# Weighted sums of both query halves in one bank, copied and turned once per unit; at most one operand load behind a store of maxima

## The reference

```python
scores = jnp.einsum('bhqd,bhkd->bhqk', q, k)          # / sqrt(8), masked
attn = jax.nn.softmax(scores, axis=-1)
out = jnp.einsum('bhqk,bhkd->bhqd', attn, v)
```

## Time and profile before

| what | value |
|---|---|
| median of three runs | 1235.33 us |
| profiled execution | 1236.83 us, its span 1234.9 us |
| TensorE busy | 1122.0 us, 91% |
| VectorE / ScalarE / GpSimd busy | 935.3 / 735.9 / 447.5 us |
| first attention, 188.7 to 687 us | TensorE busy 489.0 of 498.3 us |
| second attention, 776 to 1000 us | TensorE busy 210.5 of 224.0 us |
| granted clock, mean | 0.955 |

### The profile page before, as it was taken

The page is one execution under the profiler, slowest core; times in us unless marked ns, Lnnn a source line. Parts: engine busy times, 40 slices in busy tenths (PEclk is TensorE's granted clock), DMA queues, the critical chain, the costliest instruction groups (busy, mean ns, idle before and its releaser), DMA issues. The chain is left out here.

```text
span 1234.9 us, 22211 instructions
## 1 busy us (share of the span) xinstructions
PE 1122.0 (91%) x7511; PEld 614.9 (50%) x7518; DVE 935.3 (76%) x2098; ACT 735.9 (60%) x1148; POOL 447.5 (36%) x714
## 2 busy tenths in 40 slices
PE   4668879999999999999998697799999989999997
PEld 2345663344444444343443374444444448888874
DVE  7979988688888888888884372877787636777776
ACT  3557640666666666666666453356666667787762
POOL 6002220142323332332222120387776622566630
PEclk9989996899999999999999897799999989999999
DMA  4322790003302130212000013222222253687542
GB/s 137 96 84 64 113 125 2 19 27 108 101 13 93 41 116 23 82 55 85 28 2 2 1 54 86 67 64 61 64 65 61 58 169 127 188 258 245 163 122 83
DMA packets 94975, 103.52 MB, mean 84 GB/s; under 512 B 17217, under 2 KB 72838, under 8 KB 94864
## 3 DMA queue, kind: packets, MB, share of 16 engines
q1 hardware_dynamic: 88928, 93.09, 28.0%
q0 software_dynamic: 4992, 8.48, 2.0%
q10 hardware_dynamic: 944, 0.54, 0.2%
HBM read 64.67 MB, written 38.43 MB: 83 GB/s over the span
## 5 line engine op out<-in xcount | busy, mean ns | idle before, releaser
L1136 ACT ACTIVATE a_probs<-a_pst 128x1024 f32<-128x1024 f32 (+4 forms) x544 | 413.9, 813 | 274.9 <-PE a_pst L1084 274.3
L1160 DVE TENSOR_REDUCE a_tops<-a_ps 128x1 f32<-128x512 f32 (+9 forms) x624 | 340.9, 589 | 84.4 <-PE a_ps L1054 76.6
L992 POOL TENSOR_SCALAR_AFFINE_SELECT a_probs<-a_probs 128x256 f32<-128x256 f32 (+3 forms) x384 | 180.6, 481 | 366.8 <-ACT a_probs L1136 361.4
L1054 PE MATMUL a_ps<-kp,qp 96*128 96x512 bf16 (+9 forms) x1280 | 293.5, 307 | 0.0
L1084 PE MATMUL a_pst<-qp,kp 99*128 99x512 bf16 (+4 forms) x1088 | 259.1, 330 | 15.2 <-DMA qp<-a_top_rows 11.5
L1103 PE MATMUL a_po<-a_probs,vh 128*32 128x512 f32 (+4 forms) x2176 | 232.0, 499 | 2.6 <-POOL a_probs L992 2.5
L1160 DVE TENSOR_REDUCE a_tops_lead<-a_ps 128x1 f32<-128x512 f32 x256 | 161.6, 681 | 5.9 <-PE a_ps L1054 5.6
L1054 PEld LDWEIGHTS a_ps<-kp,qp 96*128 96x128 bf16 x1280 | 111.4, 100 | 79.1 <-DVE a_tops_lead L1160 15.5
L1051 PE MATMUL a_ps<-mask_s,identb 128*128 128x128 bf16 (+8 forms) x624 | 144.1, 234 | 6.8 <-PEq L1254 4.4
L1084 PEld LDWEIGHTS a_pst<-qp,kp 99*128 99x128 bf16 (+1 forms) x1088 | 91.8, 99 | 110.9 <-ACT a_probs L1136 47.2
L1738 POOL DMA_INDIRECT chosen_rows<-e_slot_y,e_slot_x x92 | 93.3, 1014 | 97.0 <-DVE e_slot_y L1958 75.3
(11 more groups left out here) (314 smaller groups left out, 1624.0 us busy)
## 6 DMA issues: line engine op xcount, KB each, us to landing
e_slot_w<-weight_parts SPq DMA_DIRECT2D x23, 1024.0 KB
qp<-q_parts SPq DMA_DIRECT2D x64, 96.0 KB
slot_rows<-empty_row SPq DMA_DIRECT2D x4, 1495.0 KB, 27.2
e_slot_x<-slot_rows SPq DMA_DIRECT2D x23, 260.0 KB, 3.1
a_raw<-in_wraw SPq DMA_DIRECT2D x18, 256.0 KB, 3.6
weight_parts<-first_rows SPq DMA_DIRECT2D x9, 512.0 KB, 3.0
weight_parts<-a_cut SPq DMA_DIRECT2D x9, 512.0 KB, 3.1
qp<-q_parts SPq DMA_DIRECT2D x64, 64.0 KB
```

Source lines behind the costliest of these rows:

```text
L992: pool.affine_select(out=seen, in_=seen, compare_op=ALU.is_ge, fill=0.0, base=m0, pattern=[[0, 2], [1, mw]], channel_multiplier=-1 if laye ...
L1054: last = pe.matmul(bank[:, i * room:i * room + w], sb["qp"][slot][0:KROWS, j, f["qt"] * P:(f["qt"] + 1) * P], sb["kp"][slot][0:KROWS, j // ...
L1136: act.activation(probs[local % RING][0:st["rows"], 2 * part:2 * part + 2, st["off"]:CHUNK], p_st[part][0:st["rows"], :, st["off"]:CHUNK], ...
L1160: dve.tensor_reduce(out, scores, AX.X, ALU.max).then_inc(s["banks_read"], 1)
```

## The change

Both query halves of a unit are summed in one bank. A value tile's row has 48 columns a head instead of 32: 16 of zero, then the 8 values and a one, then zeros. The first half's steps read columns 16 to 47, the second half's columns 0 to 31, so the first half lands in rows 0 to 15 and the second in rows 16 to 31 of each head's 32. The bank starts at the unit's first step and is done at its last, so there are one copy, one turn of four matmuls and one reciprocal (of 32 columns a partition, where it was 16) for a unit, and two scaling products. The "end" entry of the first half stays for what GpSimd and SyncE hang on it. The planner's rules follow, and it appends only one load behind a turn of the maxima. To make room for the wider tiles, four weights are kept only through the first two stages.

```diff
+VAT = 16
+VROW = VAT + VW
...
-            if 2 * sums + 1 < pairs and not (outs and self.steps[sums % S]["last"]):
+            if 2 * sums + 1 < pairs and not (outs and sums % S == S - 1):
                 ready.append((max(pe, exp_end[2 * sums], exp_end[2 * sums + 1],
-                                  sums_free if self.steps[sums % S]["first"] else 0)
+                                  sums_free if sums % S == 0 else 0)
...
-                for done in emptied:
+                if emptied:
+                    done = emptied.pop(0)
                     order.append(("next_load", done, 0, 0))
                     loaded[done + GROUPS] = pe + LOADED_US
-                emptied = []
             if what == "turn_out":
                 pe = start + 4 * LOAD_US
-                m, c = outs.pop(0)
-                banks[mine] = dve = max(dve, pe + PASS_US) + 4 * REDUCE_US
-                order.append(("turn_out", m, c, 0))
+                banks[mine] = dve = max(dve, pe + PASS_US) + 8 * REDUCE_US
+                order.append(("turn_out", outs.pop(0), 0, 0))
...
-                    act = sums_free = copied_end[m, st["c"]] = max(act, sums_end[sums]) + 4 * REDUCE_US
                     order.append(("end", m, st["c"], 0))
-                    outs.append((m, st["c"]))
+                if sums % S == S - 1:
+                    act = sums_free = copied_end[m] = max(act, sums_end[sums]) + 4 * REDUCE_US
+                    outs.append(m)
...
-        inv_sum = tmp("inv_sum", [P, CT, GH])
+        inv_sum = tmp("inv_sum", [P, CT, GH, T // CHUNK])
...
-                last = pool.tensor_copy(dst[:, 0:full, :, 0:D],
+                last = pool.tensor_copy(dst[:, 0:full, :, VAT:VAT + D],
...
-            def turn_out(n, c, use):
-
-                pe.wait_ge(s["o_copied"], since["o_copied"] + 2 * n + c + 1)
+            def turn_out(n, use):
+
+                pe.wait_ge(s["o_copied"], since["o_copied"] + n + 1)
...
-                if st["first"]:
-                    pe.wait_ge(s["o_copied"], since["o_copied"] + 2 * n + st["c"])
+                    pe.wait_ge(s["o_copied"], since["o_copied"] + n)
                 pe.wait_ge(s["exp_done"], since["exp_done"] + 2 * (local + 1))
                 if st["mask"]:
                     pe.wait_ge(s["unseen_zeroed"], since["unseen_zeroed"] + 2 * (M * n + geo.masked.index(k) + 1))
+                v0 = VAT if st["c"] == 0 else 0
                 for j in range(GH):
 
-                    last = pe.matmul(p_o[VW * j:VW * (j + 1), st["off"]:CHUNK], sb["vh"][n % 2][0:st["rows"], st["kt"], j, :],
+                    last = pe.matmul(p_o[VW * j:VW * (j + 1), st["off"]:CHUNK], sb["vh"][n % 2][0:st["rows"], st["kt"], j, v0:v0 + VW],
                                      probs[local % RING][0:st["rows"], j, st["off"]:CHUNK],
-                                     start=st["first"], stop=st["last"], tile_position=(0, VW * j),
+                                     start=k == 0, stop=k == S - 1, tile_position=(0, VW * j),
                                      skip_group_check=True)
...
-                if what == "end":
-
-                    act.wait_ge(s["pv_done"], since["pv_done"] + S * n + 1 + max(
-                        i for i, st in enumerate(geo.steps) if st["c"] == k))
+                if what == "end" and k == T // CHUNK - 1:
+
+                    act.wait_ge(s["pv_done"], since["pv_done"] + S * (n + 1))
...
-            def scale_out(n, c, use):
+            def scale_out(n, use):
 
                 turned = filled_bank(use)[:, :].rearrange("p (t j w) -> p t j w", t=CT, w=VW)
                 dve.wait_ge(s["banks_read"], read(use - 1))
-                dve.reciprocal(inv_sum[:, :, :], turned[:, :, :, D]).then_inc(s["inverse_done"], 1)
-                dve.wait_ge(s["inverse_done"], since["inverse_done"] + 2 * n + c + 1)
+                dve.reciprocal(inv_sum[:, :, :, :], turned[:, :, :, D:D + VAT + 1:VAT]).then_inc(s["inverse_done"], 1)
+                dve.wait_ge(s["inverse_done"], since["inverse_done"] + n + 1)
                 b, g = n // GROUPS, n % GROUPS
-                out = sb["o"][:, b * (T // P) + c * CT:b * (T // P) + (c + 1) * CT, g * GH * D:(g + 1) * GH * D]
-                dve.tensor_tensor(out.rearrange("p t (j d) -> p t j d", d=D), turned[:, :, :, 0:D],
-                                  inv_sum[:, :, :].unsqueeze(3).broadcast_to([P, CT, GH, D]), ALU.mult)\
-                    .then_inc(s["banks_read"], 1)
+                for c in range(T // CHUNK):
+                    out = sb["o"][:, b * (T // P) + c * CT:b * (T // P) + (c + 1) * CT, g * GH * D:(g + 1) * GH * D]
+                    last = dve.tensor_tensor(out.rearrange("p t (j d) -> p t j d", d=D),
+                                             turned[:, :, :, VAT * c:VAT * c + D],
+                                             inv_sum[:, :, :, c:c + 1].broadcast_to([P, CT, GH, D]), ALU.mult)
+                last.then_inc(s["banks_read"], 1)
...
-            sb["vh"] = [attentions.enter_context(nc.sbuf_tensor(f"vh{i}", [P, T // P, GH, VW], F32)) for i in range(2)]
+            sb["vh"] = [attentions.enter_context(nc.sbuf_tensor(f"vh{i}", [P, T // P, GH, VROW], F32)) for i in range(2)]
...
+            with ExitStack() as firsts:
+                for name, shape in (("wqkv", [P, 3 * E]), ("wg", [P, INNER]), ("wu", [P, INNER]), ("wd", [P, 3, P])):
+                    sb[name] = firsts.enter_context(nc.sbuf_tensor(name, shape, F32))
+                first_projection(nc, io, sb, dram)
+                quantised_ffn(nc, sb, dram)
```

More of the change, by code:

```diff
@@ L328, in _ @@
             for n in range(2):
-                pool.memset(sb["vh"][n][:, :, :, D:D + 1], 1.0).then_inc(shaped, 1)
+                pool.memset(sb["vh"][n][:, :, :, VAT + D:VAT + D + 1], 1.0).then_inc(shaped, 1)
             pool.tensor_copy(sb["iota8"][:, :], sb["iota8i"][:, :]).then_inc(shaped, 1)
@@ L852, in counted_before @@
     units = B * GROUPS
-    ends = T // CHUNK * units
     uses = sum(what in BANK_USES for what, *_ in geo.order())
@@ L856, in counted_before @@
                   exp_done=2 * units * geo.S, unseen_zeroed=2 * units * len(geo.masked), pv_done=units * geo.S,
-                  v_staged=units, o_copied=ends, inverse_done=ends)
+                  v_staged=units, o_copied=units, inverse_done=units)
     return {name: START + layer * count for name, count in layer0.items()}
@@ L980, in stage @@
                     rows = geo.keys - full * P
-                    last = pool.tensor_copy(dst[0:rows, full, :, 0:D],
+                    last = pool.tensor_copy(dst[0:rows, full, :, VAT:VAT + D],
                                             v_all[0:rows, v0 + full, f0:f0 + GH * D]
@@ L1119, in _ @@
                 if what == "turn_out":
-                    turn_out(n, k, use)
+                    turn_out(n, use)
                 use += what in BANK_USES
@@ L1220, in _ @@
                 if what == "turn_out":
-                    scale_out(n, k, use)
+                    scale_out(n, use)
                 use += what in BANK_USES
@@ L2016, in build @@
         keep("o", [P, TILES, E])
-        for name, n in (("wqkv", 3 * E), ("wout", E), ("wq1", E), ("wk1", E), ("wv1", E), ("wo1", E), ("bo", E),
-                        ("gw", EXPERTS), ("gbias", EXPERTS), ("wg", INNER), ("wu", INNER), ("minus_half", TILES), ("minus_magic", 1),
+        for name, n in (("wout", E), ("wq1", E), ("wk1", E), ("wv1", E), ("wo1", E), ("bo", E),
+                        ("gw", EXPERTS), ("gbias", EXPERTS), ("minus_half", TILES), ("minus_magic", 1),
                         ("ident", P), ("iota8", EXPERTS)):
@@ L2023, in build @@
         keep("wconv", [P, STRIDE, E])
-        keep("wd", [P, 3, P])
         keep("iota8i", [P, EXPERTS], I32)
@@ L2072, in build @@
             sb["k1_parts"] = attentions.enter_context(nc.sbuf_tensor("k1_kept", [P, PARTS, KEYS1], BF16))
-            first_projection(nc, io, sb, dram)
-            quantised_ffn(nc, sb, dram)
+            with ExitStack() as firsts:
[3 more added lines that the diff above has]
+                quantised_ffn(nc, sb, dram)
             attention(nc, io, sb, dram, 0)
```

## The result

The changed kernel takes 1250.8 us (five runs, 1248.4 to 1258.3) against 1235.3 us: ratio 1.0124, 95% interval 1.0102 to 1.0145. It is slower, and the time lies above the range of 1214 to 1237 us (I had 1226.2). The profiled execution is the slowest of the five, 1258.3 us; the profiled one of before took 1236.8.

What follows compares the result with a forecast made beforehand. TensorE was taken to set the pace in both attentions. Second attention -7.4, first 0, ends -2.2, loads 0 and value tile +0.5 sum to -9.1 us: 1226.2 us against a median of 1235.3, range 1214 to 1237.

Steps and rivals of the forecast that it cites:

- Second attention, what takes the place: Second attention: TensorE's issue and waits in the new order, -0.57 us per unit, -7.4 us over 13 steady intervals.
- the lock of VectorE and GpSimd: First stage: shared port pair locked during the value tiles' longer memset; by that rule the sum would be 0.5 us higher.
- The two waits for exponentials: Second attention: score pairs at a unit's second and third step wait for ScalarE, 0.30 and 0.35 us.
- First attention, "I take 0": First attention: new waits offset the saved turns, net -0.1 to +0.2 us per two units, taken as 0; ends -7 and +7.
- my added waits: First attention: TensorE's waits for store, exponentials and copy grow by 1.2 to 1.3 us per two units, over seven periods.
- sign of being wrong in kind: Profile after: weighted sums waiting for GpSimd, or the first stage ending over 1.1 us later, would show this.
- Turns, copies, scaling: Both attentions: 32 fewer turns take 16.0 us from TensorE's queue; 32 fewer copies and reciprocals matter only through waits they end.
- Ends: First and last units of each attention: uncovered copies, waits that go and one more scaling product, -2.2 us for all.
- One load behind a store: First attention: two operand loads now follow every other store; taken as 0, between -1 and +1 us.
- Wider value tile: First stage: GpSimd's memset grows from 2.12 to 3.18 us, costing VectorE 0 to 1.06 us; 0.5 taken.
- rival (c): Unit boundaries: probabilities run dry, an exponential uncovered at every second one, +14 us on the forecast, 1240 us; chance 0.13.
- Its sentence on GpSimd: Second attention: GpSimd pauses only 0.66 and 0.92 us a unit; masks ready only some 0.7 us before the sum needing them.

Runs made afterwards that it cites:

- e11: Changed kernel with a unit's last fill and VectorE's tail one weighted sum earlier in the second attention; 1236.6 us, ratio 0.9997 to the kernel before.
- e15: e11 plus GpSimd's cuts of the second half's end two weighted sums later in the first attention; 1242.8 us, ratio 1.0014 to the kernel before.
- e1: Changed kernel's arithmetic (one bank, copy and turn per unit) in the order and load rule of the kernel before; 1232.6 us, ratio 0.9970.
- e3: Kernel before with only the rule on loads changed (one behind a store); 1235.9 us, ratio 0.9995.
- e9: Changed kernel with GpSimd's cuts of the first half's end two weighted sums later in the first attention; 1248.1 us, ratio 1.0099.
- e12: e1 with, in the second attention, the maxima's turn before the output's and the next weighted sum before the next unit's first pair; 1218.9 us, ratio 0.9866.

## Why the prediction was wrong

*The step that failed* is the first of "Second attention, what takes the place": it counts TensorE's issue from one turn of maxima to the next and has no term for the turn's own wait. I looked at what follows the turn, not at what it needs. In the kernel before it came 0.68 us behind the tail's end. The new order left 2.4 us of work between the last fill and the turn where there were 2.7, and put the tail beside two selects, which made it 2.3 us long from its start to its end where it was 0.85. That is a wait of 0.83 us for most units (12.5 us over 13 waits) and 13.61 us a unit where I expected 12.62. I had read GpSimd's gaps only for what they mean to weighted sums, and weighed the lock of VectorE and GpSimd only for one memset.

*The counted terms held where this wait is gone.* I expected 12.62 us a unit (13.19 less 0.57). e11, with the changed order and an undisturbed tail, has 12.70. The two waits for exponentials are there in size too. In one unit of e11:

```profile
890.65 0.29 PE L1063 MATMUL a_ps<-kp,qp 96*128 96x299 bf16 x1
891.08 0.28 PE L1093 MATMUL a_pst<-qp,kp 99*128 99x128 bf16 x2
...
891.39 0.30 PE L1063 MATMUL a_ps<-kp,qp 96*128 96x342 bf16 x1
891.85 0.60 PE L1093 MATMUL a_pst<-qp,kp 99*128 99x512 bf16 x2 [0.15 <-ACT a_probs L1145]
```

By starts, with 0.42 ns a column, the pairs wait 0.30 and 0.32 us, where I had 0.30 and 0.35. The list of waits shows only 2.3 us over thirteen pairs, as it leaves out the part that a matmul's recorded length covers. So this part of the forecast was right in its terms and wrong in its list.

*First attention, "I take 0".* +7.0 us in the profile. 4 us are the three cuts beside the tail (e15), again the turn's own wait. The rest is close to the count: e15 against e1, the same arithmetic in the new and the old order, is 9.2 us, where my added waits (1.2 to 1.3 us, seven times) were 8.4 to 9.1. Against the kernel before, 2.3 us are left in place of 0. Some of it is sums that wait for GpSimd, 2.1 us in e15 and 0.2 in the kernel before (240 to 670 us). This I had named as a sign of being wrong in kind; it is real, but small.

*Turns, copies, scaling.* Their worth is visible in e1: 6.9 us in the first attention, nothing in the second, where a shorter queue only uncovers the 3.36 us from turn to pair. That this time is fixed was right for nearly all units of the second attention, and wrong for part of the first. Where VectorE copies the turned maxima at once (0.29 us behind the turn's start) the pair comes 3.3 to 3.6 us behind the turn. At every other boundary of the first attention the changed kernel's copy starts 0.96 us behind it, after VectorE's reduces, and the pair comes 4.0 to 4.2 us behind it and has been waited for (turn at 398.90, copy at 399.87, pair at 402.97).

*Ends*, taken as -2.2 us: nothing of it shows. From the last turn of maxima of the first attention to the first of the second and from the last one to the end of the span it is 122.0 and 252.0 us before, 122.1 and 251.9 in e1, 123.8 and 252.4 in the changed kernel. The first of the two varies from 119.6 to 123.8 between profiles, so a gain of 1 us could hide in it.

*One load behind a store*, taken as 0: right (e3).

*Wider value tile.* The memset takes 2.97 us for 2.12. The feed-forward's first matmul starts at 80.3 to 80.6 us in the five kernels with two banks, and at 81.1 to 82.3 in the twelve with one, 1.0 us later on average where I took 0.5 with 1.06 at most. The first turn of maxima comes at 212.0 to 213.0 and at 213.6 to 215.6, 1.8 us later on average; where the other 0.8 arises is open. The tile was not tried alone; the change also places other tensors anew.

*What this leaves.* The profiled execution is 21.4 us longer: 11.3 in the second attention where I had 7.4 less, 7.0 in the first, 0.8 ahead of them, 1.8 between them and 0.4 behind. The median is only 15.5 us longer. The step of 2.58 us, with its wait and the lower clock behind it, fits the difference: e9, with the same order in the second attention, does not have it and takes 203.1 us there for 209.0. Which of the unprofiled runs have it no trace shows. Without any held tail the new order would not have paid what I forecast either: 452.5 (e15) and 192.2 us (e11) in the attentions against 450.2 and 197.7, with 1.8 for the start, are 1.4 us less by this estimate, not 9.1.

*Rivals.* The time came out slower, as rival (c), but not by its mechanism: the pairs' waits for exponentials are those of the forecast, without the 14 us that it put on top (the list of waits has 3.9 us more than before). Its sentence on GpSimd came nearest, though it has weighted sums waiting for masks (3.7 us more) and not VectorE's tail.

The Trainium skill ("SBUF — State Buffer", "SBUF: two separate sides") says that the shared port pair belongs for the whole instruction to whichever starts first, a GpSimd instruction or a VectorE step in a two-port mode or with two SBUF inputs (the latter only against a GpSimd instruction that reads SBUF), and that the other blocks fully. The rows agree: 0.19 us becomes 1.20, 0.54 or 1.14 us beside selects and cuts that read SBUF, ending within 0.06 us of GpSimd's work. The page does not say that a held step can wait for more than one instruction, as the step of 1.20 us does. My prediction used this rule once and not for the small steps that something waits for. By an estimate from the rows, 13 waits of 0.83 us are 10.8 us and turn the -9.1 into +1.7: the sign, but not the size.

## What to carry to other kernels

A step of 0.2 us on the path can cost 1.2 us when its neighbour engine happens to work beside it: after reordering, look up what GpSimd does during each short VectorE step that something waits for. Count a reordered unit from both sides, what follows the pivotal instruction and what it needs. Removing work under a latency gained nothing in the second attention until something else was put there (e1), and 10.7 us came from moving two pieces of TensorE's work (e1 to e12). A long wait can cost twice: 2.84 us of idle TensorE were followed by several us at the lower clock.

## What the runs showed of the hardware

VectorE's reduces, which read PSUM, are untouched by GpSimd. In the attentions of the changed kernel's profile, reduces of 512 columns take 685 ns on average with nothing of GpSimd's beside them (291 of them) and 684 ns with a select beside them for at least 80% of their length (31). The same holds for the reciprocal (357 ns alone, 356 with GpSimd's computing beside it for at least half) and the scaling product (286 and 284 with a select beside it). The copy of the maxima takes 208 ns alone and 220 beside an indirect transfer. Of these steps only the tail's, whose tiles all lie in SBUF, are held for long, those with one input as well as those with two. A held step can outlast more than one GpSimd instruction: 1.20 us over two selects back to back, 2.58 us over the rest of an indirect transfer, a select and a bias addition. Beside GpSimd's indirect transfers alone a step took 0.18 to 0.65 us.
